# Where the pair products of the queries are made in a Taylor attention block

## The reference

```python
normed = rms_norm(x, gamma)
q = (normed @ w_q).reshape(b, n, h, dh).transpose(0, 2, 1, 3)
kv = (normed @ w_kv).reshape(b, n, 2, h, dh).transpose(2, 0, 3, 1, 4)
k, v = (kv[0], kv[1])
q = q * dh ** (-0.5)
q = second_taylor_expansion(q)          # 1, q, and all products q_i q_j * 0.5 ** 0.5
k = second_taylor_expansion(k)
kv_state = jnp.einsum('bhnd,bhne->bhde', k, v)
k_sum = jnp.sum(k, axis=2)
den = jnp.einsum('bhnd,bhd->bhn', q, k_sum)
qk_inv = 1.0 / jnp.maximum(den, EPS)
out = jnp.einsum('bhnd,bhde->bhne', q, kv_state) * qk_inv[..., None]
return out.transpose(0, 2, 1, 3).reshape(b, n, h * dh) @ w_out
```

## Time and profile before

| | us |
|---|---|
| median of 3 runs | 711.26 |
| lowest and highest | 710.67, 712.90 |
| the profiled execution | 710.23 |
| its span, from the first to the last instruction | 708.4 |
| key pass, from the trace | about 262 to 344 |
| query pass, from the trace | about 344 to 450 |

### The profile page before, as it was taken

One profiled execution on the slowest core, in us unless ns is written; L12 is line 12 of the kernel. 1 busy time (PEld: TensorE's weight loads), 2 busy tenths in 40 slices (PEclk: granted clock), 3 DMA queues, 4 the chain that ended last, 5 costly groups with the idle time before them and its releaser, 6 DMA issues.

```text
span 708.4 us, 13478 instructions
## 1 busy us (share of the span) xinstructions
PE 510.0 (72%) x3830; PEld 373.5 (53%) x3832; DVE 425.5 (60%) x1784; ACT 332.7 (47%) x690; POOL 313.6 (44%) x329
## 2 busy tenths in 40 slices
PE   1759520278868508777899996059999999999934
PEld 1457100245545304333433433049999999999921
DVE  4789668835412237898527778874445455455447
ACT  3815510034323104455446773156666666666616
POOL 3514300057878732343001221126776766767535
PEclk9966755569978857899999998569999999999967
DMA  7401263022333351100000100021111111111155
GB/s 190 132 0 44 81 269 148 3 41 40 39 47 42 34 174 31 31 15 1 1 1 16 31 24 23 15 29 42 50 49 45 49 48 45 49 45 49 39 198 172
DMA packets 47735, 42.22 MB, mean 60 GB/s; under 512 B 15345, under 2 KB 41834, under 8 KB 47178
## 3 DMA queue, kind: packets, MB, share of 16 engines
q1 hardware_dynamic: 35770, 25.48, 11.5%
q0 software_dynamic: 10816, 15.82, 10.6%
q10 hardware_dynamic: 1104, 0.39, 0.2%
HBM read 26.23 MB, written 15.30 MB: 59 GB/s over the span
## 4 chain that ended last, share of the span: by engine, by line
PE 48%; DVE 24%; issue 10%; ACT 7%; DMA 5%; POOL 5%; ACTq 1%; DVEq 0%; POOLq 0%; SPq 0%
PE bank L1888 18%; PE bank L1909 9%; DVE st L1262 3%; PE bank L1699 3%; POOL sum_dram L676 3%; ACT arena L916 2%; PE bank L1744 2%; PE bank L1800 2%; PE bank L1734 2%; DVE st L992 2%; DVE mv L1267 2%; POOL arena L664 1%; PE bank L1833 1%; PE bank L1898 1%; DVE hit L1106 1%
## 5 line engine op out<-in xcount | busy, mean ns | idle before, releaser
L1888 PE MATMUL bank<-arena 128*128 128x128 f32 x1136 | 140.4, 277 | 0.4 <-ACT arena L967 0.4
L1888 PEld LDWEIGHTS bank<-arena 128*128 128x128 f32 x1136 | 134.2, 194 | 0.7 <-ACT arena L967 0.7
L690 POOL TENSOR_TENSOR rstd<-ve,mhalf 128x4 f32<-128x4 f32 x40 | 48.7, 1218 | 162.1 <-DVE ve L1270 116.0
L1523 DVE TENSOR_TENSOR arena<-arena,bank 128x512 f32<-128x512 f32 x71 | 48.8, 688 | 81.8 <-PE bank L1888 81.8
L744 POOL DMA_INDIRECT y_dram<-arena,sidx x71 | 70.1, 987 | 44.3 <-DVE arena L1528 41.0
L953 ACT ACTIVATE arena<-wgu 128x1024 f32 x71 | 75.0, 1058 | 26.6 <-PE bank L1888 26.2
L736 POOL DMA_INDIRECT arena<-x3row_dram,gidx x71 | 69.0, 972 | 36.7 <-issue 20.7
L1909 PE MATMUL bank<-w,arena 128*128 x568 | 75.1, 275 | 0.0
L1909 PEld LDWEIGHTS bank<-w,arena 128*128 128x128 f32 x568 | 69.1, 192 | 0.2 <-issue 0.2
L959 ACT ACTIVATE arena<-bank 128x512 f32<-128x512 f32 x71 | 42.4, 597 | 42.6 <-PE bank L1888 42.6
L676 POOL DMA_INDIRECT sum_dram<-arena,idx x32 | 50.7, 1586 | 15.2 <-issue 7.9
(11 more groups left out here) (324 smaller groups left out, 1018.7 us busy)
## 6 DMA issues: line engine op xcount, KB each, us to landing
wgu<-in_wgu SPq DMA_DIRECT2D x1, 4096.0 KB, 12.2
wgu<-y_dram SPq DMA_DIRECT2D x8, 512.0 KB, 6.3
X<-in_x SPq DMA_DIRECT2D x8, 256.0 KB, 5.6
sum_dram<-zero POOLq DMA_DIRECT2D x8, 256.0 KB, 4.2
x1row_dram<-row SPq DMA_DIRECT2D x8, 256.0 KB, 2.4
w<-in_w SPq DMA_DIRECT2D x1, 2048.0 KB, 17.3
acc<-sum_dram SPq DMA_DIRECT2D x8, 256.0 KB, 2.9
w<-in_wd SPq DMA_DIRECT2D x1, 2048.0 KB, 9.3
```

The lines of the kernel that those rows point to most:

```text
L690: nc.gpsimd.tensor_tensor(out, ve[:, u], mhalf[:, 0:J], ALU.pow).then_inc(done, 1)
L1523: nc.vector.tensor_tensor(gl[:, m.pair], sgl[:, m.pair], bank[3 + m.pair][:], ALU.mult).then_inc(f_gated, 1)
L1888: last = nc.tensor.matmul(bank[first + m.pair][:, h * P:(h + 1) * P], wnow[:, m.pair, at_:at_ + P], xrT[:, m.ring], start=True, stop=True)
```

## The change

The pair products move into the key pass. There TensorE makes them from `qT` right behind `qkv(3)` (bank 7, which the queries have just left), and ScalarE squares them between the normalisation of the next group and the copy of `xnT`; the squares of all 8 groups are kept. In the query pass the pair product and its square are gone, the second four rises wait for the first four squares alone, and the first two of the four 64-row products (`turn` 0) stand where the pair product stood, ahead of the y products. To have room for the squares, `pairs` shares one tile, `turns`, with `x1T`, `sT` and `w2`. The counts of the semaphores follow.

```diff
-        x1T = sb("x1T", [P, NB, W])
-        sT = sb("sT", [E0, NB, W])
+        turns = sb("turns", [P, GR * W])
+        x1T = turns[:, 4 * W:6 * W].rearrange("p (b w) -> p b w", b=NB)
+        sT = turns[0:E0, 6 * W:8 * W].rearrange("p (b w) -> p b w", b=NB)
+        pairs = turns[:].rearrange("p (g w) -> p g w", g=GR)
...
-        pairs = [part(4096 + HD * W, W), part(13088, W)]
...
-        w2 = sb("w2", [P, E0, 2, D])
+        w2 = turns[:, 0:4 * W].rearrange("p (e k n) -> p e k n", e=E0, k=2)
...
                     normalise(lambda j: xn[:, g.b, j], tokens(g), g.b).then_inc(d_xn, 1)
+                if m:
+                    act.wait_ge(d_qt, LEAD + 2 * m.n + 2)
+                    nc.scalar.activation(pairs[:, ds(m.place, 1)].rearrange("p o w -> p (o w)"), bank[7][:], ACT.Square,
+                                         bias=one_row[:, 0:1]).then_inc(q_t, 1)
+                if g:
                     act.wait_ge(d_xtps, LEAD + g.n + 1)
...
-                if n:
-                    act.wait_ge(q_z, LEAD + 9 * n.n + 5)
-                    nc.scalar.activation(pairs[n.b][:], bank[RISE[0]][:], ACT.Square, bias=one_row[:, 0:1]).then_inc(q_sq, 1)
...
                 qkv(3)
+                if m:
+                    pe.wait_ge(q_t, LEAD + 2 * m.n + 1)
+                    nc.tensor.matmul(bank[7][:], pairs_of[:], qT[:, ds(m.place, 1)].rearrange("p o w -> p (o w)"), start=True,
+                                     stop=True).then_inc(d_qt, 1)
                 accumulate(m, 1)
...
+                def state_x_of(g, turn):
+                    for u in range(2):
+                        half = slice(64 * u, 64 * u + 64)
+                        k_ = (turn + u + 1) % 2
+                        last = nc.tensor.matmul(bank[3 + u][:], state_x[half, g.b, k_], (qT if k_ else pairs)[half, g.place],
+                                                start=False, stop=(turn == 1), skip_group_check=True)
+                        if turn == 1:
+                            last.then_inc(q_out, 1)
...
-                if n:
-                    pe.wait_ge(q_sq, LEAD + 9 * n.n + 1)
-                    nc.tensor.matmul(bank[RISE[0]][:], pairs_of[:], qT[:, n.place], start=True, stop=True).then_inc(q_z, 1)
+                if l:
+                    state_x_of(l, 0)
                 if m:
                     pe.wait_ge(q_ot, LEAD + m.n + 1)
...
                 if l:
-                    for turn in range(2):
-                        for u in range(2):
-                            half = slice(64 * u, 64 * u + 64)
-                            k_ = (turn + u + 1) % 2
-                            last = nc.tensor.matmul(bank[3 + u][:], state_x[half, l.b, k_],
-                                                    qT[half, l.place] if k_ else pairs[l.b][half], start=False, stop=(turn == 1),
-                                                    skip_group_check=True)
-                            if turn == 1:
-                                last.then_inc(q_out, 1)
+                    state_x_of(l, 1)
                 if n:
-                    pe.wait_ge(q_sq, LEAD + 9 * n.n + 5)
+                    pe.wait_ge(q_sq, LEAD + 8 * n.n + 4)
                     rise(1)
```

More of the change, by code:

```diff
@@ L886, in key_pass @@
                 if m:
-                    act.wait_ge(d_qt, LEAD + m.n + 1)
+                    act.wait_ge(d_qt, LEAD + 2 * m.n + 1)
                     nc.scalar.activation(qT[:, ds(m.place, 1)].rearrange("p o w -> p (o w)"), bank[7][:],
@@ L914, in square @@
                 def square(c, out, where):
-                    act.wait_ge(q_z, LEAD + 9 * n.n + c + 1)
+                    act.wait_ge(q_z, LEAD + 8 * n.n + c + 1)
                     nc.scalar.activation(out, bank[where][:], ACT.Square).then_inc(q_sq, 1)
@@ L932, in query_pass @@
                     for c, h in enumerate(ROUND[1]):
-                        square(5 + c, squares[:, h], RISE[c])
+                        square(4 + c, squares[:, h], RISE[c])
             each_group(query_pass, 2)
@@ L1756, in key_pass @@
                     if not early(m, 1):
-                        pe.wait_ge(q_t, LEAD + m.n)
+                        pe.wait_ge(q_t, LEAD + 2 * m.n)
                     nc.tensor.matmul(bank[7][:], wqkv[:, NKV:], xnT[:, m.b], start=True, stop=True).then_inc(d_qt, 1)
@@ L1791, in _ @@
             pe.wait_ge(d_kv, LEAD + 2 * J * GR)
-            pe.wait_ge(q_t, LEAD + GR)
+            pe.wait_ge(q_t, LEAD + 2 * GR)
             def query_pass(at):
@@ L1807, in apply @@
                                          squares[:, h], start=True, stop=False, skip_group_check=True)
+                def state_x_of(g, turn):
[6 more added lines that the diff above has]
+                            last.then_inc(q_out, 1)
                 if n:
                     if not early(n, 1):
-                        pe.wait_ge(q_sq, LEAD + 9 * n.n)
+                        pe.wait_ge(q_sq, LEAD + 8 * n.n)
                     rise(0)
                 if l:
-                    pe.wait_ge(q_sq, LEAD + 9 * l.n + 9)
+                    pe.wait_ge(q_sq, LEAD + 8 * l.n + 8)
                     apply(l, 1)
```

## The result

The changed kernel takes 704.84 us (median of 12 runs, 703.23 to 709.23); the kernel before took 712.0 us beside it (12 runs, 710.09 to 719.44). The ratio is 0.9889 with a 95% interval of 0.9864 to 0.9914: faster by 7.9 us, 6.1 to 9.7 (the two medians lie 7.2 apart). The forecast was 706.9 in a range of 704.9 to 709.6, so the direction holds and the time lies just under the range. The profiled execution took 704.95 us (span 703.1) against 710.23 (span 708.4). Busy time says nothing here: TensorE went from 510.0 to 510.2 us, VectorE from 425.5 to 425.4.

The account below looks back on a forecast made before the run. VectorE was taken to pace the key pass, a TensorE-ScalarE ring the query pass. Terms +0.36 - 2.60 - 0.57 + 0.65 - 1.06 - 1.14 = -4.36 us gave 705.87 profiled, 706.9 as time; range 704.9 to 709.6.

Parts of the forecast that it names:

- -2.24: Key pass to the first rise: +0.36 us for the last group's product and -2.60 for two clock falls taken as gone.
- free, as costed: Key pass: added product (1.02 us) hidden in groups 0 to 6, added square (0.69 us) hidden before the copy of xnT.
- the loop named as late next: Query groups 2 and 3: y, statistics, power, logits add, residual adds, transposes back bind at 9.51 us; -1.14 for two.
- The hole: Query groups 2 and 3: the 1.21 us before y holds turn 0, at 1.16 us, so y would not be later.
- the clock term of "Query pass, group 0": TensorE's new 2.1 us wait before the second rises may lower the clock: +0.65 us, bounds 0 and 1.80.
- the +0.36 for the last group: Key pass, group 7: added product of 1.02 us against a wait of 0.66 leaves +0.36 us on the path.
- the offset in "The sum": Whole kernel: median before (711.26) lies 1.03 us above the profiled execution; 705.87 thus became a time forecast of 706.9.
- The falls stay: Rival: key-pass clock falls remain; sum -1.76 or -2.41 us, time 708.9 to 709.5; chance 0.22.
- More than forecast: Rival: no new fall, groups 2 and 3 at 9.22 us: 705.7, with other low stretches down to 705; chance 0.10.
- Eaten: Rival: VectorE binds from query group 2, taking most gains of groups 1 to 3; falls staying, 710.2 to 711.3; chance 0.09.
- slower: Rival: new key-pass square delays xnT, up to 0.69 us in each of 7 groups: +2.4, 713.7; chance 0.07.
- The loop with choices: Query pass from group 4's first residual add: VectorE's loop with choices (10.64 us) or the y loop binds; gain 0, at most 0.2.

Follow-up runs that it names:

- product_only: Kernel before plus the pair product also made in the key pass, result unused, query pass as before: 708.32 us, ratio 0.9943 to the kernel before.
- one_piece: Changed kernel with turn 0 moved back behind y, the four 64-row products in one piece: 706.35 us, ratio 0.9913 to the kernel before.
- rise_between: Changed kernel with the next group's first rises between the two halves of the transposes back, from group 2 on: ratio 0.9942 to the kernel before.
- fill_first: Changed kernel with one unused pair product behind the first rises of query-pass group 0 alone: ratio 0.9869 to the kernel before.
- turn_only: Kernel before with turn 0 moved ahead of the y products, the pair product kept in the query pass: 715.39 us, ratio 1.004 to the kernel before.
- product_twice: Changed kernel with the key-pass pair product made twice in a row, first result overwritten: ratio 0.9887 to the kernel before.
- square_twice: Changed kernel with the key-pass square made twice, once into a buffer nobody reads: ratio 0.9893 to the kernel before.
- warm_start: Changed kernel with four unused 320-column products on TensorE ahead of the key pass: ratio 0.9903 to the kernel before.

## Where the prediction held and where it failed

The forecast of 706.9 was 2.06 us too high: 0.92 in the sum (705.87 for the profiled execution, which took 704.95) and 1.14 in the offset that was added to it. Of the 0.92, 0.73 lie in groups 0 and 1 of the query pass, 0.32 in the key pass and 0.26 in the groups behind, against 0.39 the other way in stages that the change doesn't touch.

**Right.** The product in the gap takes time off the key pass, as product_only shows, and in the first pair of profiles the size is near: -2.56 against -2.24. Fall by fall it is in part luck. Groups 2 and 5 gained 1.80 and 0.95; a fall of 0.82 came in group 4, where the prediction had none left; and group 0, which was in no term, was 0.59 shorter (9.41 against 10.00). The last isn't shown to come from the change: with the same key pass one_piece and rise_between have 9.98 and 9.88 us there. What is steady is the whole pass: 72.29 to 72.93 us in five profiles (after twice, one_piece, rise_between, fill_first), 75.43 to 76.72 in the three of before. The pair product and its square in the key pass are free, as costed.

*Query pass.* Group 0: the second rises follow the first by 345.20 - 341.93 = 3.27 us instead of 3.84, which is the 0.57 forecast, behind an idle time of 2.13 (2.1 forecast). Group 1: removed product, 7.26 us; what the 8.94 of before had beyond that is 1.06 and a low-clock part, below. Groups 2 and 3: 9.51 forecast, 9.50 measured, and by the loop named as late next: the adds start 379.29 - 371.55 = 7.74 us behind the first rise (7.75 forecast) and the next rises follow 381.05 - 379.29 - 1.12 = 0.64 behind their end (0.64 forecast). Groups 5 and 6: 10.63 between their adds (10.64).

*The hole.* The hole before y is used to its end and not over it: turn 0 takes 375.32 - 374.20 = 1.12 us (1.16 allowed), and y starts 3.77 us behind the first rise as before. The 0.06 beyond 1.06 can be the wait for the copy of oT, which ends at 375.26; in turn_only, where that copy is done earlier, turn 0 takes 378.22 - 377.16 = 1.06. So two halves of 1.06 (here 376.44 to 377.50 for the second) stand against 1.92 in one piece: the split costs 0.20 us. The Trainium skill (TensorEngine Tiling (Array Packing), Key Properties) says that a change of the tiling mode drains TensorE. In this trace y is not later; whether the 0.20 is such a drain no run separates.

**Failed: the clock term of "Query pass, group 0".** It asked only what the new wait would add (+0.65) and not what would become of the low stretch that was already there behind the forming of the state. Both have rows. The new one came: from the second rises to the first product of the forming it takes 349.17 - 345.20 = 3.97 us, where before it was 350.88 - 348.31 = 2.57: +1.40. The old one went: from the apply to the next rise and on to the next apply, 0.99 + 1.07 us instead of 1.86 + 1.70: -1.50. So -0.10 stands where +0.65 was written: in the first pair the two groups gained 1.71 instead of 0.98, which is 0.73 of the 0.92. In the other two executions of before the two groups took 1.35 and 1.22 longer (23.18 and 23.05 against 21.83), so that the ledger has -2.57.

The size of the term isn't settled. Seven profiles have the changed first rises without a filler beside them: the low stretch is on the second rises alone in four (after twice, one_piece, rise_between: 20.12 or 20.13 us for the two groups), later alone in two (product_twice and square_twice: 21.46 and 24.10), in both places in one (warm_start: 22.57). Their mean is 21.23, against 22.85 of the five profiles with the old ones (before three times, product_only 23.10, turn_only 23.09): -1.62, which would put the clock term at 0. In six of the seven one stretch stands in place of the other, and not beside it as the sum had it; what decides its place and length is open.

**Failed: the +0.36 for the last group.** From its first key product to the first rise it took 344.47 - 338.21 = 6.26 us before and 341.93 - 335.66 = 6.27 after: 0.01. The sum took the product's busy time (1.02) against the idle time in brackets (0.66), and both were the wrong figure. The product adds 0.86: the accumulates start 340.24 - 338.63 = 1.61 us behind the products of qkv(3) (L1737) instead of 341.93 - 341.18 = 0.75. The room is 0.85: before, the 48 accumulates and the wait among them took 344.47 - 341.93 = 2.54, and in one piece the 48 take 341.93 - 340.24 = 1.69. A second product has no room left and costs 0.85 (product_twice: 7.12).

**Failed: the offset in "The sum".** The 1.03 us between the median and the profiled run was carried over as a constant. It is not a constant: after the change it is -0.1 (704.84 and 704.95). In part it was the low clock that an ordinary run of before has and the profiled one had less of, and so the same miss as in group 0, seen in the runs: the second profile of before is 1.19 us longer than the first (711.42), and groups 0 and 1 alone are 1.35 longer. The third is 5.35 longer, of which 2.45 lie in the key pass and these two groups and the rest in stages that the change doesn't touch. That the falls of the key pass add to it isn't shown: the 4.1 us of product_only have an interval that holds the 2.60 of the earlier trace rows.

**The rivals.** "The falls stay": one of the key falls stayed in both executions of after (10.41 and 10.40 us in group 4), so the case is real but small. "More than forecast" gave 705 to 705.7, and the time came out just under it, but for one of its reasons only: groups 2 and 3 did not reach 9.22 and a new fall did come; what it named last, a share of the other low stretches of the two passes, is what went behind the forming of the state. "Eaten" and "slower" are out; the doubled square shows the second to have been far away. The loop with choices gives back a little of what groups 2 to 4 save: in group 5, 10.23 us from rise to rise (396.55 to 406.78) became 10.64 (390.61 to 401.25).

## What to carry to other kernels

Where TensorE's clock falls in a profile, price it over several executions: here the low stretch at the start of the query pass changed its place and its length (20.12 to 24.10 us for two groups) in kernels whose code is the same there, so one profile with a filler and one without it can't show what the filler does. The product that was moved into a wait paid twice here, once for the work it took off the other place (1.06 us in group 1) and once for the clock (some 3 us in the key pass). When two edits share one hole, as the pair product and turn 0 do here, each alone can give nothing or a loss, and the number to compare is the start of what follows the hole.

## What was not expected of the hardware

- With four unused products of 320 columns, a pair product in group 0 and one at the state, one execution (701.98 us) had the granted clock at 1.00 through the key pass and the first two groups of the query pass; each of the two parts tried alone (warm_start, fill_first) had a low stretch in its profile. The clock of ordinary executions of this kernel in these stages was not seen.
- The fall of the clock doesn't follow one gap: in after, the accumulates wait 1.73 us in the third group and 1.72 in the fifth (313.05); only the fifth has the fall, and there the first batch still runs at 0.71 and the second at 1.23. In turn_only a key pass of unchanged code had a low clock in six groups behind group 0.
- The two 64-row products on the two halves of the rows run side by side: both start within 0.01 us (374.20 and 374.21) and take 0.69 us in the first of their two passes, and the two together cost what one full product does: 1.06 us to the next instruction (376.44 to 377.50; one full product in the earlier trace rows).
